# One core, layer 2 of a two-layer network: expert rows gathered by an index table through three places in SBUF, in place of a scatter to HBM

## What is computed

```python
    xn = _layernorm(x, axis=-1)
    s = _L1_attn_ref(xn)                      # attention across the batch
    g = _silu(_L1_ffn_ref(xn, gate_w, w1, w2, w3))
    x = x + s * g
    # _L1_ffn_ref:
    probs = jax.nn.softmax(xt @ gate_w.T, axis=-1)
    top_vals, top_idx = jax.lax.top_k(probs, K)          # K = 2 of E = 8
    act = jax.nn.silu(h1) * h3                           # h1 = x w1^T, h3 = x w3^T, F = 800
    y = sum over the two experts of weight * (act w2^T)
```

## Time and profile before

| | |
|---|---|
| median of the runs | 1500.3 us |
| the profiled execution: its time, its span | 1499.98 us, 1498.2 us |
| `across_batch`, from its first instruction to the end of the last addition | 762.0 to 872.4 us |
| `experts`, first product to the last | 881.4 to 1441.3 us |
| `combine` | 1445.2 us to the end |
| busy: TensorE, VectorE, ScalarE, GpSimd | 90%, 47%, 38%, 41% of the span |

### The profile page before, as it was taken

How to read it: one execution, slowest core, us unless ns; L and a number is a source line. 1 busy time by engine, 2 the same in 40 slices (tenths; PEclk the granted TensorE clock), 3 DMA queues, 4 the chain that set the end, 5 groups by cost and what they waited for, 6 DMA issues and landing times. The chain is left out here.

```text
span 1498.2 us, 25022 instructions
## 1 busy us (share of the span) xinstructions
PE 1346.3 (90%) x7870; PEld 1147.5 (77%) x7871; DVE 702.3 (47%) x1622; ACT 565.6 (38%) x1775; POOL 612.0 (41%) x518
## 2 busy tenths in 40 slices
PE   6989899999999999999885679999999999999940
PEld 6934487878787878887654569999999999999930
DVE  6452376666676766667636432223223222232236
ACT  3421276655556656655543321111212211112124
POOL 0010155444444545455426345172662617441135
PEclk9999899999999999999987789999999999999975
DMA  8025710000000000000015465373773828555247
GB/s 290 1 84 163 280 71 15 15 14 14 14 14 14 14 23 19 14 14 16 8 60 207 163 228 184 106 241 115 231 245 95 271 69 290 178 161 182 72 130 253
DMA packets 67069, 171.47 MB, mean 114 GB/s; under 512 B 6448, under 2 KB 15040, under 8 KB 66704
## 3 DMA queue, kind: packets, MB, share of 16 engines
q0 software_dynamic: 25776, 98.73, 19.8%
q1 hardware_dynamic: 35632, 61.95, 12.8%
q10 hardware_dynamic: 5616, 10.23, 1.9%
HBM read 125.26 MB, written 45.61 MB: 114 GB/s over the span
## 5 line engine op out<-in xcount | busy, mean ns | idle before, releaser
L1721 PE MATMUL bank<-expert_weights,rows_t 128*128 x1872 | 358.9, 347 | 2.1 <-DVE rows_t L1653 1.6
L1721 PEld LDWEIGHTS bank<-expert_weights,rows_t 128*128 128x128 f32 x1872 | 340.2, 189 | 6.1 <-issue 2.9
L989 ACT ACTIVATE room<-bank,room 128x256 f32<-128x256 f32 (+1 forms) x512 | 208.8, 415 | 115.5 <-DVE room L902 115.4
L1017 POOL TENSOR_TENSOR room<-room 128x1024 f32<-128x1024 f32 (+1 forms) x128 | 187.9, 1468 | 119.1 <-DVE room L879 119.1
L753 PE MATMUL bank<-room 96*128 (+2 forms) x1024 | 189.1, 327 | 0.0
L1665 DVE TENSOR_TENSOR x_keep<-x_keep,bank 128x400 f32<-128x400 f32 x78 | 44.5, 571 | 303.9 <-ACT x_keep L1608 302.6
L1131 POOL TENSOR_TENSOR expert_weights<-x_keep,expert_weights 128x1600 fp32r<-128x1600 f32 (+2 forms) x49 | 160.2, 3270 | 54.2 <-DMA expert_weights<-w 53.9
L753 PEld LDWEIGHTS bank<-room 96*128 96x128 f32 x1024 | 159.0, 191 | 13.7
L1744 PE MATMUL bank<-expert_weights,act_t 128*128 x702 | 165.6, 389 | 1.0 <-ACT act_t L1613 1.0
L1028 POOL TENSOR_TENSOR room<-room 128x256 f32<-128x256 f32 x128 | 93.1, 728 | 172.3 <-DVE room L963 171.1
L1744 PEld LDWEIGHTS bank<-expert_weights,act_t 128*128 128x128 f32 x702 | 131.5, 188 | 25.6 <-issue 1.3
(11 more groups left out here) (235 smaller groups left out, 1770.9 us busy)
## 6 DMA issues: line engine op xcount, KB each, us to landing
x_keep<-w POOLq DMA_DIRECT2D x28, 800.0 KB, 5.1
expert_weights<-w POOLq DMA_DIRECT2D x28, 800.0 KB, 6.5
x_keep<-w POOLq DMA_DIRECT2D x14, 768.0 KB, 5.7
expert_weights<-w POOLq DMA_DIRECT2D x14, 768.0 KB, 7.4
rows_by_expert<-room SPq DMA_DIRECT2D x1, 9984.0 KB, 29.1
x_keep<-rows_by_expert SPq DMA_DIRECT2D x39, 256.0 KB, 3.9
results_by_row<-x_keep ACTq DMA_DIRECT2D x39, 256.0 KB, 4.5
room<-wo SPq DMA_DIRECT2D x16, 512.0 KB, 5.7
```

What stands on the lines that cost most here:

```text
L989: last = sc.activation(Pr[:, m % 4, hh, 0:w], scores_bank(m)[:, w * hh:w * hh + w], ACT.Exp, bias=nb[:, par, hh:hh + 1], accum_out=sm[:, p ...
L1017: g.tensor_tensor(pr, pr, rs[:, one[1] % 2].unsqueeze(2).broadcast_to([P, 4, w]), ALU.mult).then_inc(normed, 1)
L1721: last = mm(psum(2 * hf + w)[:, 0:HF], xgT[:, par, of_x, P * k:P * k + P], W[:, ds(off + (of_w * SLOT + (k * 2 + w) * FF + hf * HF), HF)], ...
```

## The change

1. The zero fill of `rows_by_expert` and the scatter are gone. SyncE stores the 16 normalised row tiles to a new HBM tensor `rows_normalised`. An index table (`s.index`: for each block and place, which row) is computed inside the rounds: VectorE compares slots with block numbers and places (`find_blocks`, `name_tiles`, `find_places`), ScalarE scales once, TensorE sums 32 small products (`index`), VectorE writes the table (`write_index`). The block tables that stood after the rounds move into round 5.
2. GpSimd gathers blocks 0 and 1 straight into `xg` at the end of `across_batch`. Blocks 2 to 38 are gathered in `experts` into three places in SBUF (`Passing`), stored from there to `rows_by_expert` by GpSimd, and loaded by SyncE as before.
3. The first expert: three raw places, chunks 0 to 2 have their high part loaded by GpSimd's DMA; ScalarE makes the high parts of chunks 3 to 6 one after another between the router's exponential and round 0; GpSimd makes the low parts of 0, 1 and, after the slots, of 2, 3, 5, 6; VectorE that of 4. Nothing of it is left to `experts`.
4. The router's folding product with a constant becomes 16 turns by TensorE and two reductions by VectorE.

```diff
+def gather_rows(s, b, to, landed):
+    s.nc.gpsimd.indirect_dma_start(
+        out=to, out_offset=None, in_=s.xn,
+        in_offset=bass.IndirectOffsetOnAxis(ap=s.index[:, b:b + 1], axis=0)).then_inc(landed, 16)
+class Passing:
...
+    def gather(self):
+        i, s = self.gathered, self.s
+        if i + 2 < NBLK:
+            if i >= PLACES:
+                self.pool.wait_ge(s.rows_there[i % PLACES], 16 * (i // PLACES))
+            gather_rows(s, i + 2, self.places[i % PLACES], s.rows_got[i % PLACES])
+            self.gathered += 1
+    def keep(self):
+        s = self.s
+        while self.kept < self.gathered:
+            i = self.kept
+            self.pool.wait_ge(s.rows_got[i % PLACES], 16 * (i // PLACES + 1))
+            self.pool.dma_start(s.xs[P * (i + 2):P * (i + 3), :], self.places[i % PLACES]).then_inc(
+                s.rows_there[i % PLACES], 16)
+            self.kept += 1
...
-            sp.dma_start(s.xs.rearrange("(n p) h -> p n h", p=P),
-                         zeros.unsqueeze(1).broadcast_to([P, NBLK, D])).then_inc(s.blank, 16)
...
+            def keep_rows(t):
+                sp.wait_ge(xn_ready, t + 1)
+                sp.dma_start(s.xn[P * t:P * t + P, :], X[:, t]).then_inc(xn_stored, 16)
+            for c in range(3):
+                bring_chunk(sp, s, 0, c, raw[:, c % 3]).then_inc(s.raw0_in[c % 3], 16)
+            for t in range(NT):
+                keep_rows(t)
+            for c in range(3, NCH):
+                sp.wait_ge(pool_low, c - 2)
+                bring_chunk(sp, s, 0, c, raw[:, c % 3]).then_inc(s.raw0_in[c % 3], 16)
...
+            for c in EARLY_LOW:
+                take_low(c)
             pool.wait_ge(slots_ready, 1)
-            for t in range(NT):
-                for k in range(2):
-                    nc.gpsimd.indirect_dma_start(
-                        out=xs, out_offset=bass.IndirectOffsetOnAxis(ap=s.slots[:, t, k:k + 1], axis=0),
-                        in_=X[:, t], in_offset=None).then_inc(sorted_, 16)
-            pool.wait_ge(sorted_, 16 * 2 * NT)
+            for c in LATE_LOW:
+                take_low(c)
+            pool.wait_ge(index_steps, 7)
+            for b in range(2):
+                gather_rows(s, b, s.xg[:, b], s.first_in[b])
...
-            high_of(0)
             act.wait_ge(p_ex, 1)
             sc.activation(p, p, ACT.Exp).then_inc(p_exd, 1)
-            high_of(1)
+            high_of(3)
+            high_of(4)
+            high_of(5)
+            high_of(6)
...
+                if r == 1:
+                    high, low = parts_of(s, 4, 0)
+                    dve.wait_ge(first_high, 2)
+                    v.tensor_tensor(low, raw_of(4), high, ALU.subtract)
+                if r == 0:
+                    find_blocks()
+                if r == 1:
+                    name_tiles()
+                if 1 <= r < 5:
+                    find_places(r - 1)
+                if r == 5:
+                    write_index()
+                    block_tables()
...
             bring_raw(0)
-            pool.wait_ge(first_w2, NCH - KT_PER_D - 1)
+            rows = Passing(s, pool, passing)
+            for _ in range(PLACES):
+                rows.gather()
             for stored in s.messages_stored:
                 pool.wait_ge(stored, 16)
             bring_high(0)
+            rows.keep()
             for j in range((E - 1) * NCH):
...
                 pool.wait_ge(high_in[j % 2], 16 * (j // 2 + 1))
-                at, rows, n = CHUNKS[c]
-                low_of(s, c, stage[0:rows, j % 2, 0:n], e % 2 * 2 * SLOT).then_inc(s.converted, 1)
+                rows.keep()
+                rows.gather()
+                at, n_rows, n = CHUNKS[c]
+                low_of(s, c, stage[0:n_rows, j % 2, 0:n], e % 2 * 2 * SLOT).then_inc(s.converted, 1)
+                rows.keep()
+                rows.gather()
+                if c + 1 == NCH:
+                    rows.keep()
+                    rows.gather()
+                    rows.keep()
                 if more and c + 1 == NCH:
                     bring_high(j + 1)
...
-            with sp.Fori(0, (NBLK - 3) // 2) as i:
+            for b in range(2, NBLK):
+                sp.wait_ge(s.rows_there[(b - 2) % PLACES], 16 * ((b - 2) // PLACES + 1))
+                sp.wait_ge(x_turned, b - 1)
+                load(b, b % 2)
```

More of the change, by code:

```diff
@@ L38 @@
 PT_RING = 8
+PLACES = 3
 EARLY_ROWS = NT - 2
@@ L148, in build @@
         s.xn_ready = s.sem("rows_normal")
-        s.raw0_in = [s.sem(f"raw0_in{i}") for i in range(2)]
+        s.raw0_in = [s.sem(f"raw0_in{i}") for i in range(3)]
         s.messages_stored = [s.sem(f"messages_stored{i}") for i in range(4)]
@@ L1214, in _ @@
             nc.gpsimd.memset(zerosb, 0.0).then_inc(zeroed, 1)
+            for c in DMA_HIGH:
+                at, rows, n = CHUNKS[c]
+                bring_chunk(pool, s, 0, c, s.W[:, at:at + n]).then_inc(high0_in[c], 16)
             for t in range(POOL_XP):
@@ L1304, in _ @@
             dve.wait_ge(lt, 1)
-            step.then(v.tensor_copy(p, psum(7)[:, 0:P].rearrange("p (t e) -> p t e", t=NT)))
+            for hf in range(2):
+                quarters = s.bank[2 + hf][:, :].rearrange("p (t k e) -> p t e k", t=NT // 2, k=4)[:, :, 0:E]
+                last = v.tensor_reduce(p[:, NT // 2 * hf:NT // 2 * hf + NT // 2], quarters, AX.X, ALU.add)
+                step(last)
+            step.wait()
             step.then(v.tensor_reduce(top, p, AX.X, ALU.max))
@@ L1415, in _ @@
             route(3)
-            pe.wait_ge(consts2_in, 16)
             for t in range(NT):
                 pe.wait_ge(logit_out, t // 4 + 1)
-                last = mm(psum(7)[:, E * t:E * t + E], LT[:, P * t:P * t + P], const("fold4"), start=True, stop=True)
+                last = tr(psum(4 + t // 4)[:, P * (t % 4):P * (t % 4) + P], LT[:, P * t:P * t + P], ident)
             last.then_inc(lt, 1)
@@ L1473, in message, with index @@
                     last.then_inc(a_msg, 1)
+            def index():
+                pe.wait_ge(own_named, 1)
+                pe.wait_ge(index_steps, 6)
+                for i in range(2 * NT):
+                    last = mm(psum(7)[:, 0:2 * NBLK].rearrange("p (w b) -> p w b", w=2), place_hit[:, i], named[:, i],
+                              start=(i == 0), stop=(i == 2 * NT - 1))
+                last.then_inc(indexed, 1)
             pe.wait_ge(mask_ready, 2)
@@ L1524, in _ @@
             pool.sem_inc(s.converted, 1)
-            for c in range(KT_PER_D + 1, NCH):
-                at, rows, n = CHUNKS[c]
-                low_of(s, c, s.raw0[0:rows, c % 2, 0:n], 0).then_inc(first_w2, 1)
             def bring_raw(j):
```

171 lines of the change are left out of this document (105 added, 66 removed).

## The result

The changed kernel takes **1539.0 us** (median of 4 runs, 1536.6 to 1549.8), the kernel before beside it 1499.5 us: a ratio of 1.0287, 95% interval 1.0260 to 1.0314, 39.6 us slower. The forecast was 1514, its range 1486 to 1545. The measured time lies in the range, and the sign and the mechanism came out; the size did not: +14.2 was forecast, nearly three times as much came.

What follows compares the result with a forecast made beforehand. TensorE was taken as busy except for a 28.4 us stall beside GpSimd's scatter in `across_batch`, with GpSimd the engine to watch in `experts`. -20 (earlier start) + 28.8 + 5.4 = +14.2 on 1499.98 gave 1514 us, range 1486 to 1545.

Steps and rivals of the forecast that it cites:

- 2, scatter's stall: Rounds of `across_batch`: removing the scatter ends the stall of all engines, -28.4 us, bounds 0 and 28.4.
- 3, round 0's exponential: Ahead of round 0: ScalarE's four high parts move its exponential from 798.98 to 806, +7 us, bounds +2 and +12.
- 4, index in the rounds: Rounds: VectorE's index tables, small steps and moved block tables add +8 us, bounds +3 and +13.
- 5, seam: Last addition to first turn in `experts`: tables gone, blocks 0 and 1 already in `xg`, -5.6 us.
- 5, clock of the first 24 products: Start of `experts`: with a shorter idle TensorE keeps part of the 1.8 us its first 24 products lose, -1 us.
- 6, late experts: `experts`: GpSimd's chunk step of 10.7 us makes second, third, fourth expert late by 6.7, 14.6, 7.5: +28.8 us.
- 6, restarts: `experts`: after each of three stops TensorE loses what its first 24 products lose, 3 x 1.8 = +5.4 us.
- 7, block 2's rows: Row loads in `experts`: the extra trip through HBM is not late once started, 0; otherwise one 4.5 us load.
- Term 1: Layer 1: the zero store and its memset leave, where TensorE does not wait for them, 0.
- GpSimd keeps up: Rival, chance 0.22: in `experts` the chunk step is 9.3 us or less, 1490 us; decides at about 9.6 us.
- The stall stays: Rival, chance 0.06: the stall in the rounds has another cause or code loads behind row stores, no saving, 1542 us.
- Gathers crawl: Rival, chance 0.12: in `experts` gathers wait behind both weight loads, a chunk step of 12.7 us, 1541 us.

Runs made afterwards that it cites:

- runs 7: Two edits of the kernel before: second-choice scatters left out (16 of 32 stay), 1470.4 us; each scatter replaced by a plain store, 1472.8 us; one run each.
- keep_one_later: Changed kernel with each store of a gathered block moved behind the next gather in GpSimd's list: 1509.0 us, ratio 1.0065 to the kernel before.
- syncengine_stores: Changed kernel with the 37 stores moved from GpSimd to SyncE and SyncE's 37 row loads to ScalarE: 1499.5 us, ratio 1.0027 to the kernel before.
- straight_stores: Kernel before with each of its 32 scatters replaced by a plain store to 128 consecutive rows, same queue: 1472.8 us, one run.
- experiment 3: Changed kernel with ScalarE's high parts of chunks 4, 5 and 6 moved into rounds 0, 1 and 3: 1541.3 us, ratio 1.0270 to the kernel before.

## Why the prediction was wrong in size and right in kind

Its steps against the two profiled executions (1499.98 and 1539.52 us, 39.5 apart):

| step | forecast | measured | from |
|---|---|---|---|
| 2, scatter's stall | -28.4 | -28.4 | no "remote" wait left; runs 7 |
| 3, round 0's exponential | +7 | +2.4 | 801.37 - 798.98 |
| 4, index in the rounds | +8 | +8.9 | 801.37 to 855.24 is 53.9; before 73.4, less the stall's 28.4 |
| 5, seam | -5.6 | -5.4 | 855.24 to 856.22 against 6.4 |
| 5, clock of the first 24 products | -1 | +0.6 | 6.98 against 6.34 |
| 6, late experts | +28.8 | **+50.9** | 6.7, 14.6, 7.5 against 13.2, 22.1, 15.6 |
| 6, restarts | +5.4 | +5.8 | 6.36 + 6.47 + 6.63 - 3 x 4.55 |
| 7, block 2's rows | 0 | +3.0 | 878.19 |

The measured column sums to 37.8 of 39.5 us. (Term 1 was put at 0: `across_batch` began 0.6 us earlier, less than executions of one kernel differ by.) Term 3 came out smaller because the slots were there at 791.2 us instead of 794 and the high part of chunk 5 could start at 799.5.

**The step that failed is term 6, and in it two waits.** The step was put at 10.7 us; the ten steps between the first and sixth low parts of the second and third expert took 12.3 on average:

```profile
870.29 3.67 POOL L1169 TENSOR_TENSOR expert_weights<-x_keep,expert_weights 128x1600 fp32r<-128x1600 f32 x1
...
933.82 3.43 POOL L1169 TENSOR_TENSOR expert_weights<-x_keep,expert_weights 128x1536 fp32r<-128x1536 f32 x1
...
970.02 3.67 POOL L1169 TENSOR_TENSOR expert_weights<-x_keep,expert_weights 128x1600 fp32r<-128x1600 f32 x1
...
1029.39 3.42 POOL L1169 TENSOR_TENSOR expert_weights<-x_keep,expert_weights 128x1536 fp32r<-128x1536 f32 x1
```

63.5 and 59.4 us against 53.5 forecast for five steps. The issue times held (a gather 1.0 plus 0.3, a store 0.57, the low part 3.7). The wait behind the weight loads was 2.0 us on average instead of 1.6, the wait behind the low part 1.5 instead of 0.3 (sums of the ten: 20.4 and 15.3 us). That is 16.7 us more in ten steps, and 10.0 + 5.9 = 15.9 is what the steps were late by. With 1.2 us in the second expert's start and the steps of the fourth, the three experts' last low parts came 11.5, 6.4 and 7.1 us later than worked out, 25.0 in all; TensorE was itself some 3 us later, as long as it had waited for block 2, so its waits grew by 22.1.

The error was in the sentence that the low part covers the second gather "but for 0.3". It took the landing from rows of weights and of `combine`. In the ten steps the store of a gather that was issued behind the weight loads started 4.6 to 9.4 us after that gather, 6.2 on average, and of one issued ahead of them 4.0 to 6.1 us after it, 4.3 on average. The high loads themselves took 7.7 to 7.9 us (medians) to land between 963 and 1041 us, where the forecast had 6.7. Whether the place behind the loads on their queue or the traffic makes the gather late was not tried.

**A small price, paid by an engine without room.** The 25 us are 1.6 us a step over the 16 steps that carry gathers. All of them counted, since the spare time was already spent in the forecast.

**Term 7** was priced at 0 "once started"; at the start it was 3.0 us, within the 4.5 that the text gave for that case. GpSimd's timeline shows block 2's gather and the store that waits for it:

```profile
857.51 0.99 POOL L210 DMA_INDIRECT x_keep<-rows_normalised,tables  x1 [0.30 <-issue]
...
864.19 1.16 POOL L234 DMA_DIRECT2D rows_by_expert<-x_keep  x2 [2.58 <-DMA x_keep<-rows_normalised,tables]
```

The gather, issued behind the second expert's first raw load, is stored 6.7 us later, and only then can SyncE load the rows.

**The rivals.** "GpSimd keeps up" did not happen; its point of decision, a step of 9.6 us, came out a little lower, as far as kernels with other lists can show it: in keep_one_later steps of 10.3 us end 10 us above the kernel before, in syncengine_stores steps of 9.1 us 3 us above. "The stall stays" is refuted: term 2 came in full. So the result that the Trainium skill's rule ("Runtime: NRT & Kernel Launch", instruction fetch mechanics) gave, term 2 equal to 0, did not come about; runs 7 put the stall on the indirect scatters, and no run shows whether it is code that was waited for. "Gathers crawl" gave 1541 us for a step of 12.7: it had the time nearly right, with a chance of 0.12 that was too low, since the bounds of the step (9.0 to 14) held its value as well as the forecast's. Its mechanism is the nearer one too: the step was 12.3 us, and the gather behind the weight loads was the late one.

## What to carry to other kernels

Work moved onto an engine that another engine waits for is priced by where it stands: the same 37 gathers and stores cost 61 us with two in each step, and 12 with one in each step of the second and third expert and 20 of the 37 behind an expert's last chunk. A transfer that passes through a few places has a rate of places over the time that one stays taken (landing, store, landing of the store, and what the issuing engines add): here three over 13 us. Count that beside the issue times, and when a wait is taken away look which of the two comes next. Measure the landing of a transfer in the stretch where it will be issued, behind what will stand ahead of it on its queue.

## What was not expected of the hardware

**The stall beside a scatter is a trickle.** TensorE's timeline of the kernel before, inside the stall:

```profile
835.66 0.37 PE L1443 MATMUL bank<-room 128*128 128x128 f32 x1 [1.75 <-issue]
...
838.44 0.37 PE L1443 MATMUL bank<-room 128*128 128x128 f32 x1 [2.41 <-issue]
...
840.55 0.26 PE L1444 MATMUL bank<-maskb,identb 128*128 128x128 bf16 x1 [1.74 <-issue]
```

One product of 0.3 to 0.4 us every 2 to 3 us, in a group of four that otherwise runs without a gap, waiting for nothing that the trace names. Where 16 or 32 indirect scatters follow each other, TensorE stops some 13 to 15 us after the first and goes on between 3 us before the last is issued and 4 us after it; with runs of 8 ScalarE still waits up to 7.7 us for "remote". Plain stores of the same bytes from the same queue do not cause it. What the engines wait for stays open. For the prediction's guess, code, the traces have little: in the kernel before, a packet of an instruction queue is seen at 812 to 813 us, as the stall begins, and the next only after 854, so none where the stall ends; and straight_stores has one between 812 and 815 us without a stall.

**VectorE beside GpSimd's low part.** The 1248-column pass took 4.69 us beside it and 1.45 us alone (experiment 3), and ended 1.3 us after the low part, about its own length. The Trainium skill, "SBUF — State Buffer", section on the two separate sides, says that these two engines share a port pair as an exclusive lock, held for a whole instruction, which a VectorE instruction with two inputs in SBUF needs against a GpSimd instruction that reads SBUF. Both are of that kind here, and the two rows agree.
